# Index transfers behind x's first half, and VectorE's first edge steps behind two low halves, in a two-layer graph kernel

## What is computed

```
feat = concat([x[src], x[dst]], axis=1)             # per edge, 2048 wide
e_hh = relu(feat[:128]    @ W_hh + b_hh)            # first 128 edges
e_oo = relu(feat[128:768] @ W_oo + b_oo)            # next 640 edges
e_ho = relu(feat[768:]    @ W_ho + b_ho)            # the other 7424 edges
logit = concat(e_hh, e_oo, e_ho) @ W_a + b_a        # one number per edge
alpha = softmax of logit over the edges with the same dst
z = segment_sum(alpha * x[src], dst)
new = relu(concat([x, z]) @ (W_hn for nodes < 64, else W_on) + b)
x1 = layernorm(x + new)
# second layer: h = x1 @ W, attention over the same edges, elu, residual, layernorm
```

## Time and profile before

| | |
|---|---|
| time, median of 3 runs | 348.26 us (347.84 to 349.52) |
| profiled execution, first to last instruction | 345.9 us |
| PE busy | 325.6 us, 94% |
| DVE busy | 290.3 us, 84% |
| ACT busy | 195.6 us, 57% |
| POOL busy | 116.4 us, 34% |
| HBM traffic | 182 GB/s over the span |
| granted TensorE clock, mean | 0.990 |

### The profile page before, as it was taken

The page is one execution under the profiler, slowest core; times in us unless marked ns, Lnnn a source line. Parts: engine busy times, 40 slices in busy tenths (PEclk is TensorE's granted clock), DMA queues, the critical chain, the costliest instruction groups (busy, mean ns, idle before and its releaser), DMA issues.

```text
span 345.9 us, 4739 instructions
## 1 busy us (share of the span) xinstructions
PE 325.6 (94%) x1496; PEld 250.8 (73%) x1496; DVE 290.3 (84%) x415; ACT 195.6 (57%) x306; POOL 116.4 (34%) x128
## 2 busy tenths in 40 slices
PE   7899999999999999999999999999899999979980
PEld 7678887677644788588888888888686676758730
DVE  0999999973999979899999999988888877894545
ACT  3755396202043346588888888737149576821355
POOL 4200061084000840079999999720001200060000
PEclk9999999999999999999999999999999999999996
DMA  6999599789999996003030000023498886000003
GB/s 225 402 406 408 235 310 389 246 264 235 300 363 286 375 372 217 0 0 123 3 121 2 0 3 1 2 61 123 169 350 290 321 328 243 2 0 1 0 0 121
DMA packets 17654, 63.10 MB, mean 182 GB/s; under 512 B 2250, under 2 KB 2252, under 8 KB 17376
## 3 DMA queue, kind: packets, MB, share of 16 engines
q1 hardware_dynamic: 13536, 50.07, 39.1%
q0 software_dynamic: 2096, 8.74, 8.7%
q10 hardware_dynamic: 2000, 4.00, 3.5%
HBM read 59.64 MB, written 3.16 MB: 182 GB/s over the span
## 4 chain that ended last, share of the span: by engine, by line
DVE 45%; PE 43%; ACT 5%; DMA 2%; issue 2%; SPq 0%; ACTq 0%; DVEq 0%
DVE ps L1033 25%; PE ps L1227 12%; PE ps L1276 8%; DVE W_lo L796 5%; PE ps L1434 5%; PE ps L1505 4%; PE ps L1246 3%; DVE lo_in_raw L796 3%; PE ps L1442 2%; DMA W_raw<-in_L_gnn_W_oo_dram 2%; PE ps L1537 2%; PE ps L1469 2%; DVE tile_val L815 1%; PE ps L1308 1%; PE ps L1290 1%
## 5 line engine op out<-in xcount | busy, mean ns | idle before, releaser
L505 ACT CAST W_hi<-W_raw 128x1024 fp32r<-128x1024 f32 x62 | 63.0, 1045 | 58.6 <-DMA W_raw<-in_L_gnn_W_ho_dram 28.4
L1033 DVE SCALAR_TENSOR_TENSOR ps<-ps,wa_bc 128x1024 f32<-128x1024 f32 x73 | 86.4, 1261 | 1.3 <-PE ps L1392 1.3
L796 DVE TENSOR_TENSOR W_lo<-W_raw,W_hi 128x1024 fp32r<-128x1024 f32 x54 | 65.1, 1238 | 10.3 <-ACT W_hi L505 8.3
L1392 PE MATMUL ps<-A_tab,oh 128*128 x146 | 52.1, 438 | 0.8 <-DVE ps L1033 0.8
L1227 PE MATMUL ps<-W_hi,xT_hi 128*128 128x512 f32 x112 | 45.9, 410 | 1.0 <-DVE W_lo L796 0.9
L1392 PE MATMUL ps<-B_tab,oh 128*128 x146 | 45.9, 395 | 0.0
L1227 PE MATMUL ps<-W_lo,xT_hi 128*128 128x512 f32 x112 | 43.7, 390 | 0.0
L1227 PE MATMUL ps<-W_hi,xT_lo 128*128 128x512 f32 x112 | 34.6, 390 | 0.0
L454 POOL TENSOR_SCALAR sc<-sc 128x256 f32<-128x256 f32 x37 | 32.6, 882 | 3.2
L452 POOL TENSOR_TENSOR sc<-irow,keys 128x256 f32<-128x256 f32 x37 | 23.7, 641 | 26.5 <-PE ps L1399 26.0
L1392 PEld LDWEIGHTS ps<-B_tab,oh 128*128 128x128 f32 x146 | 27.4, 188 | 6.2 <-issue 0.5
(11 more groups left out here) (283 smaller groups left out, 585.4 us busy)
## 6 DMA issues: line engine op xcount, KB each, us to landing
W_raw<-in_L_gnn_W_ho_dram SPq DMA_DIRECT2D x8, 1024.0 KB, 5.2
W_raw<-in_L_gnn_W_hh_dram SPq DMA_DIRECT2D x8, 1024.0 KB, 8.6
W_raw<-in_L_gnn_W_hn_dram SPq DMA_DIRECT2D x8, 1024.0 KB, 4.8
W_raw<-in_L_gnn_W_on_dram SPq DMA_DIRECT2D x8, 1024.0 KB, 5.2
W_raw<-in_L_gnn_W_oo_dram SPq DMA_DIRECT2D x7, 1024.0 KB, 12.2
W_raw<-in_L_gnn_W_dram SPq DMA_DIRECT2D x4, 1024.0 KB, 4.9
key_rows<-key_rows_scratch POOLq DMA_DIRECT2D x1, 2304.0 KB, 13.8
table_scratch<-tabs ACTq DMA_DIRECT2D x2, 1024.0 KB, 6.4
```

The source lines that it names most:

```text
L505: sa.copy(halves(n)[0], W_raw[:, n // 2 % NS, n % 2, :]).then_inc(hi_made, 1)
L796: v.tensor_tensor(lo, W_raw[:, n // 2 % NS, n % 2, :], hi.bitcast(F32), ALU.subtract).then_inc(lo_made, 1)
L1033: v.scalar_tensor_tensor(acc, acc, 0.0, wa_bc[:], ALU.max, ALU.mult, accum_out=keys[:, t, 2:3]).then_inc(reduced, 1)
L1392: ins = mm(acc[:, n * 512:(n + 1) * 512], oh[:, t // 2 % 2, k, t % 2 * P:(t % 2 + 1) * P], tab[:].rearrange("p q d -> p (q d)")[:, n * 512 ...
```

## The change

ACT's six index transfers are moved. Before, they were ACT's first instructions. Now the small warm-up copy comes first, then a wait for x's first half, then the two transfers of `edges`; the four of `st_col` come behind `x_high` of xT0b and before `high(1)`. On DVE the four steps on the edges move behind `low(1)` and `x_low` of xT1, `low(2)` comes before `cls_oh`, `low(3)` before the running count. On PE chunk 3 now comes before the sums of `tot`.

```diff
         @block.scalar
         def _(act):
             sa = nc.scalar
+            act.wait_ge(eps_made, 1)
+            sa.copy(warm[:, 0:1], eps_ln[:])
+            act.wait_ge(x_in[0], 16)
             for k, v in enumerate((src, dst)):
                 act.dma_start(edges[:, k, :], v[E_ST:E].rearrange("(p j) -> p j", p=P)).then_inc(edges_in, 16)
-            for k, v in enumerate((src, dst)):
-                act.dma_start(st_col[:, k, 0:1], v[0:E_HH].rearrange("(p j) -> p j", p=P)).then_inc(indices_in, 16)
-                act.dma_start(st_col[:, k, 1:], v[E_HH:E_ST].rearrange("(p j) -> p j", p=P)).then_inc(indices_in, 16)
-            act.wait_ge(eps_made, 1)
-            sa.copy(warm[:, 0:1], eps_ln[:])
...
             x_high(0, 2, "xT0a")
             high(0)
             x_high(2, 4, "xT0b")
+            for k, v in enumerate((src, dst)):
+                act.dma_start(st_col[:, k, 0:1], v[0:E_HH].rearrange("(p j) -> p j", p=P)).then_inc(indices_in, 16)
+                act.dma_start(st_col[:, k, 1:], v[E_HH:E_ST].rearrange("(p j) -> p j", p=P)).then_inc(indices_in, 16)
             high(1)
             x_high(4, KC, "xT1")
...
             x_low(2, 4, "xT0b")
+            low(1)
+            x_low(4, KC, "xT1")
             dve.wait_ge(edges_in, 32)
...
-            low(1)
-            x_low(4, KC, "xT1")
+            low(2)
             dve.wait_ge(setup_done, 1)
...
-            low(2)
+            low(3)
             link(v.tensor_tensor_scan(cum[:].rearrange("p c j -> p (c j)"), gate[:].rearrange("p c j -> p (c j)"),
                                       cls_oh[:].rearrange("p c j -> p (c j)"), 0.0, ALU.mult, ALU.add))
-            low(3)
             link(v.tensor_copy(tot[:], cum[:, :, JH - 1]))
...
-            x_dense(2, 3, G1, 0, END["ooA"])
+            x_dense(2, 4, G1, 0, END["ooA"])
             pe.wait_ge(setup_done, 1)
             pe.wait_ge(dve_step, dve_at("tot"))
...
-            x_dense(3, 6, G1, 0, END["ooA"])
+            x_dense(4, 6, G1, 0, END["ooA"])
```

## The result

The changed kernel takes 352.88 us (median of 5 runs, 351.44 to 353.42), the kernel before beside it 349.24 us (347.84 to 349.52). The ratio is 1.011, 95% interval 1.0082 to 1.0139: slower by 1.1%. The forecast had 349.9 us, 348.4 to 351.9. It was put on 348.26 us, the median of the first three runs of the kernel before; beside the changed kernel that median was 349.24. In the experiments three executions are left out of the comparisons because they ran slow: two of r9, 356.90 and 356.93 us with a granted clock of 0.975 and 0.976, and one of r8, 1848.82 us.

What follows compares the result with a forecast made beforehand. The prediction took DVE's closed chain up to low(17) to hold PE. It added 0.6 us for the st_col issues and 1.05 for the exposed edge steps to 348.26, giving 349.9 us, range 348.4 to 351.9.

Steps and rivals of the forecast that it cites:

- What bounds the kernel: DVE is a closed chain from low(1) to low(17); its shift at 12 us reaches PE at 61 us undiminished.
- x's first half: Without the index transfers ahead of it, x's first half lands 0.3 us earlier, at 5.7 instead of 6.0.
- The two edge issues on ACT: Ahead of x_high of xT0a they take 0.99 us and eat x's gain; it begins at 6.74 against 6.77.
- The four st_col issues on ACT, +0.6: Behind x_high of xT0b they take 2.1 us on ACT, so high(1) begins at 11.1 instead of 10.52.
- The edge steps, +1.05: On DVE the four steps no longer fill the hole before low(1) and are paid in the open: 1.05 us.
- x_rows, "So: nothing": PE's wait for x_rows near 28.4: fetches end at 24.9 to 30.3, taken as 27, costing nothing.
- the very shift of DVE that the forecast expected: DVE, and PE from chunk 14 on, run 1.65 us later, from the st_col issues and the edge steps.
- The rival of that name: x_rows late at PE: each microsecond counts from a landing at 30.0; 30.6 gives 350.5 us; chance 0.04.
- PE waiting for x_rows: A sign on PE that would show the prediction wrong; no size given.
- ACT's issues did not queue behind SP's: Rival that ACT's issues queue behind SP's: high(1) at 12.8, shift 3.3 us, 351.6 us; chance 0.14.
- x did not come at 4.2: Rival that x's first half lands at 4.2: DVE shifts by -0.4 us, 347.9 us; chance 0.13.

Runs made afterwards that it cites:

- r9: Changed kernel, but PE transposes x_rows behind chunk 7 instead of chunk 5; the two executions that count took 349.59 and 350.14 us, no ratio given.
- r8: Kernel before with the order of r5 and the fill of r7 together; 346.09 us, ratio 0.9929 to before.
- r3: Kernel before with only the new orders of DVE and PE, all six transfers still ACT's first instructions; 350.45 us, ratio 1.0035 to before.
- r5: Kernel before, transfers and edge steps unmoved; low(2), low(3), low(13) ahead of sorting steps, PE's chunk 3 ahead of the totals; 347.03 us, ratio 0.9939.
- r1: Changed kernel with only the four st_col transfers put back as ACT's first instructions; 349.91 us, ratio 1.003 to before.
- r4: Changed kernel with 17 unused matmuls on PE between chunk 5 and the wait for x_rows; 351.08 us, ratio 1.0067 to before.
- r6: Changed kernel with the four st_col transfers directly behind the edges, at x's first half; 353.93 us, ratio 1.0131 to before.
- r2: Kernel before with only the four st_col transfers moved behind x_high of xT0b; 350.12 us, ratio 1.0038 to before.
- r10: Changed kernel once more, unaltered, on the chip of r9; 352.49 us, ratio 1.0094 to before.
- r7: Kernel before with 11 unused matmuls in PE's 2.5 us wait for a low half in the second layer; 347.86 us, ratio 0.9966 to before.

## Why the prediction was wrong, step by step

**What bounds the kernel: right.** DVE's chain up to chunk 17 holds PE. r3 puts 1.0 us of steps into it and gets 1.02 at the tiles; r5 takes load out of it and gets 1.42.

**x's first half: right.** 0.3 us of gain forecast, 0.4 measured. Most of the slow landing was not the index transfers' doing. A rule that bears on this is in the Trainium skill, "DMA: Bandwidth & Descriptors", section "Issuing engines are not separate DMA queues": transfers issued by different engines run on the same 16 DMA engines and interleave, and issuing from several saves only the sequencer's time. The traces agree as far as this: with the edges' transfers beside it x's first half took 4.9 to 5.2 us to land, without them 4.3 to 4.8 (4.3 in r1, with the four of st_col beside it), over twelve traces.

**The two edge issues on ACT: right in effect.** x_high of xT0a at 7.15 instead of 6.77, because PE's transposes took 1.80 us instead of 1.09, not because of the issues: in r3, with the issues early, it was 7.15 as well.

**The four st_col issues on ACT, +0.6: wrong.** The price was nearly right, 1.90 us for 2.1, but the forecast put it behind x_high, from 9.03 on. The queue had begun them at 7.90, beside the copy from 7.63 on, and was done at 9.80. Against chunk 1's landing at about 9.5 they held high(1) by some 0.3 us here, by 0.5 in r9 (9.1 to 9.59), and not at all in r4. Because chunk 1 landed 1.0 us earlier, high(1) still came 0.68 us earlier. The rows of before could not show it, since there the issues were the first instructions and had nothing ahead of them; r6 shows the case in which they do hold ACT.

**The edge steps, +1.05: right**, 1.02 in r3. In the changed kernel the earlier chunk 1 takes back 0.76 of it.

**x_rows, "So: nothing": the step that failed.** It rested on three numbers. First, the landing of the fetch was put at 24.9 to 30.3 with 27 as the value taken; it was 31.2. The last st_col transfer was inside its bounds (18.58 of 15.0 to 20.4), but from there the fetches took 12.6 us instead of the 9.9 of the forecast: they came 2.45 us apart instead of 1.56, and the second took 9.85 us instead of 8.1. Both prices were taken from an execution in which the fetch ran 5 us earlier, and no margin was put on them; in r2, r4, r6 and r10 the same way took 11.8 to 13.0 us. Second, PE's time of arrival was left at 28.4; the change itself, with chunk 3 ahead of the totals, brought it to 27.36 (the new order alone, r3, to 27.65). Third, the 1.6 us that PE could give away there was the very shift of DVE that the forecast expected. With a shift of 0.3 instead, little was left. And beyond the wait, the clock was not in the sum at all: 1.65 to 2.8 us. The rival of that name had 0.04 and began to count only at 30.0. PE waiting for x_rows stood among the prediction's own signs of being wrong.

So the loss is 3.86 us of wait, less 1.07 us of earlier arrival, plus 1.44 us of low clock until chunk 6 begins (4.23), plus 0.24 of it behind, less the 0.73 us of stops that it covers: 3.74 at the tiles, 3.64 between the medians.

**The other rivals.** ACT's issues did not queue behind SP's: in the changed kernel none took over 0.51 us while SP's took 0.98 to 1.32 beside them. x did not come at 4.2; the earliest landing of its first half in any trace is 5.1 (r1).

**What stays open.** Why the second fetch takes longer when it runs later: the DMA engines moved about as much beside it in both places (399 to 414 GB/s from 15 to 23 us before, 401 to 424 from 22 to 32 in the changed kernel), and no run separates the weights' share from the st_col chain's. Why one low stretch costs 1.65 us and another 2.8 us after the same wait of 3.86 us is open too.

## What to carry to other kernels

When a small transfer is moved, follow the whole chain behind it to the first engine that waits, price every link with a margin, and compare with the consumer's new time of arrival, not its old one: moving work can shorten the path to a wait as well as lengthen the supply. A slack that exists only because another forecast delay is larger is not slack. And a wait on PE of the size of those behind which the clock fell here (2.27 us and longer) must be priced with the clock behind it; shortening it with matmuls whose results nobody uses (r4, r7) is worth trying first. Last, the base of a forecast can lie in the rarer of two groups of times: here the one traced execution had no dip, most others had.

## What the runs showed of the hardware that I had not expected

- A transfer issue on ACT's queue runs beside the engine's earlier work: four issues, 0.33 to 0.51 us each, were hidden under two copies but for some 0.3 us. Ahead of work that waits for them in order, they cost their full time (r6: 3 us of issues, x_high 1.3 us late).
- Small transfers on one queue under load land in a row: in the changed kernel the four of st_col 6.5, 7.5, 8.4 and 9.2 us after their issues, which is 1.4 us from one landing to the next. Issued 1.4 us earlier, the last landed no earlier (r6), and for issues in the same place it landed anywhere from 18.6 to 20.6 us.
- PE kept its full clock through waits of 1.27, 1.67 and 1.96 us (r4, r2, r9) and had the lower one after 2.27 and 2.36 us (both r6) and 3.86 us (the changed kernel, r10). After the 2.5 us in the second layer it fell in some executions and not in others, which makes two groups of times some 1.5 us apart, for one and the same kernel.
